# One software pipeline over all 64 units of an attention network, with the output product two slots later and the norms spread over slots

## The chip, the cores and the metric

The kernel runs on one core of a Trainium2 chip. The metric is the time of one execution on the device in microseconds, the median of several runs. The engines of the core are TensorE (PE: matmuls; PEld: its weight loads), VectorE (DVE), ScalarE (ACT), GpSimd (POOL) and SyncE (SP), whose queue issues most DMAs. Each engine works through its own queue in program order and waits on semaphores that others count up.

## The reference

The input x has 32 x 64 tokens of width 256. The first network (L0) applies two layers of cross attention with 16 heads of dimension 128, then an MLP; the second network (L1) is a smaller attention block with an MLP. The change concerns the two attention layers of L0:

```python
h = layer_norm(x)                     # mean and variance over the 256
qh = (h @ wq + bq)                    # 16 heads of 128, for 64 tokens of a batch
kh = (ctx @ wk + bk); vh = (ctx @ wv + bv)
kh, vh = concat(kh, bias_k), concat(vh, bias_v)      # 65 keys
weights = softmax(qh . kh / sqrt(128))
x = x + (weights @ vh) @ wo + bo
```

Both layers take ctx from the same context; the second layer's norm needs the first one's x, and the MLP's norm the second one's.

## The kernel before

All arithmetic is float32. A wide product is made of three matmuls on fp32r pieces (helper `three`, L166 to L170: hi x hi, hi x lo, lo x hi), so every operand exists as a rounded part (HI) and a rest (LO). `SRC_HI/SRC_LO[:, 0]` hold the transposed context, `[:, 1]` the transposed, normed x.

A **unit** is one pair of heads for one group of four token tiles (512 tokens). A layer has 8 pairs x 4 groups = 32 units, L0 has 64. One unit passes these steps: project Q and K (24 matmuls of 512 columns, PE), copy them with their bias into QT and KT (ACT, L492, L496); project V (`values(0)`, `values(1)`, 24 matmuls of 256 columns), copy it (ACT, L500), add the bias difference (POOL, L332); **scores**, 32 matmuls on 128x64 tiles into the logits (PE, L433); maximum and subtraction (DVE, L606, L615), exponential (ACT, L524), sum, reciprocal, multiply and 32x32 transposes into PRT (DVE, L567 to L578); **weigh**, 64 matmuls on 64x64 tiles of V with PRT (PE, L404) into banks 3 and 4; split into CHI (ACT, L513) and CLO (DVE, L596); **output**, 24 matmuls with wo into banks 3 and 4 again (PE), added into X (DVE, L625).

The order is written out by hand in a function `slot` for each engine. A slot has a front (unit n) and a back (unit n-1). TensorE's order is Q and K (n), values(0), weigh (n-1), values(1), scores (n), output (n-1). VectorE's is: softmax of n-1, norm, rounding of the next weights, CLO of n-1, maximum and subtraction of n, X additions of n-1. A function `slots` calls it for one layer: the first slot of a layer has no back, the last no front, so each layer ends in a drain and starts with an empty pipeline.

Weights of a pair are double buffered: SP loads W (`load`), DVE rounds it to WHI (`round_set`, L631, in slots with g = 1, where g is the group), POOL computes WLO, DV and the row sums of the output bias (`split`, L310 to L320, same slots; counted in `w_split`, for which SP's next load waits). Before the last unit of each group, POOL adds a bias row to X (L343).

The layer norm of a group of X works by stats (DVE, L88 to L97), square root (ACT, L109), reciprocal and scaling into XN (DVE, `norm_apply`, L128), transposes (PE, `norm_turn`, L137), scaling and offset from the buffer CUR into HT and SRC_HI (ACT, `norm_scale`, L152), and SRC_LO (POOL, `norm_lo`, L163). Groups 0 to 2 of the next layer's norm run in the last slots of a layer; `turning` says in which. The last group runs in slot 0 of the layer, for the MLP in the MLP's own stage.

Of the kernel before, what the change touches and what calls it, by code (L numbers as in the profile page):

```python
# [5 lines left out]
ALU = mybir.AluOpType  # L6
# [18 lines left out]
UNITS = HP * G  # L25
# [16 lines left out]
OLD = 8  # L42


def program(nc, x, ctx_in, mask, wall, vrow, borow, vech, vecm, b_fc2, qw, kw, vw, ow, out_b, w1, w2, b2, out):
    es = ExitStack()
    with es:
# [22 lines left out]
        rs = sb("rs", [P, NT])  # L70
        XN = sb("XN", [P, 2, GT, D])
# [5 lines left out]
        class Norm:  # L77
            def __init__(self, tag, src, rms, eps, prm):
                self.src, self.rms, self.eps, self.prm = src, rms, eps, prm
                self.stat, self.sqrt, self.rstd = sem(tag + "_stat"), sem(tag + "_sqrt"), sem(tag + "_rstd")  # L80
                self.xn, self.turned, self.scaled = sem(tag + "_xn"), sem(tag + "_turned"), sem(tag + "_scaled")
                self.full, self.lo = sem(tag + "_full"), sem(tag + "_lo")
                self.stats = GT if rms else 2 * GT + 1
# [56 lines left out]
        def norm_scale(e, n, k, g, banks):  # L140

            for c in range(DC):
# [5 lines left out]
                for dst, done in ((HT[:, c, :], n.full), (SRC_HI[:, 1, c, g * GTOK:(g + 1) * GTOK], n.scaled)):  # L148
                    if n.rms:
                        i = e.activation(dst, banks[c][:, :], ACT.Copy, scale=n.prm[:, c:c + 1])  # L150
                    else:
                        i = e.activation(dst, banks[c][:, :], ACT.Identity, scale=n.prm[:, c:c + 1],  # L152
                                         bias=n.prm[:, 2 + c:3 + c])
                    i.then_inc(done, 1)
# [17 lines left out]
        CUR = sb("CUR", [P, 4])  # L172

# [10 lines left out]
        norm = Norm("ln", X, False, LN_EPS, CUR)  # L184


        with ExitStack() as ph:
# [32 lines left out]

            LASTP = OLD - G

# [8 lines left out]
            cur_set = sem("cur_set")  # L231
# [7 lines left out]
            def turning(L, at, last):  # L239


                if at == 0:
                    return L, G - 1
                if last and at > LASTP + 1:
                    return L + 1, at - LASTP - 2
                return None

            def slots(e, L, slot):

                slot(L, L * UNITS, 0, L * HP, None, False)
                for i in range(0, UNITS // OLD - 1):
                    for u in range(OLD):
                        slot(L, L * UNITS + i * OLD + u + 1, u + 1, L * HP + i * 2 + (u + 1) // G, i * 2 + u // G, False)
                i = UNITS // OLD - 1
                for u in range(OLD):
                    slot(L, L * UNITS + i * OLD + u + 1, u + 1,
                         L * HP + i * 2 + (u + 1) // G if u < OLD - 1 else None, i * 2 + u // G, True)  # L260

            with nc.Block() as block:  # L262
# [27 lines left out]
                def _(e):  # L290
# [33 lines left out]
                    def slot(L, n, at, pair, hp, last):  # L324
                        g, a = at % G, (at // G) % 2
                        front, norm_now = pair is not None, turning(L, at, last)
                        if front:
                            for j in range(2):

                                e.wait_ge(v_out, 2 * n + j + 1)  # L330
                                vs = V[at % 2][:, 2 * j:2 * j + 2, :]
                                e.tensor_tensor(vs, vs, DV[a][:, :].unsqueeze(1).to_broadcast([P, 2, 2 * K]),  # L332
                                                ALU.add).then_inc(v_shift, 1)
                            if g == 1:
                                split(pair + 1, 1 - a)
                        if norm_now is not None:
                            norm_lo(e, norm, *norm_now)
                        if last and at >= G and front:

                            e.wait_ge(row_set, L + 1)  # L340
                            e.wait_ge(x_settled, 2 * n)
                            xs = X[:, (at - G) * GT:(at - G + 1) * GT, :]
                            e.tensor_tensor(xs, xs, ROW[:, :].unsqueeze(1).to_broadcast([P, GT, D]),  # L343
                                            ALU.add).then_inc(bo_added, 1)
# [4 lines left out]
                    for L in range(0, NL):  # L349
                        slots(e, L, slot)  # L350

                @block.tensor
                def _(e):
                    def slot(L, n, at, pair, hp, last):
                        g, a, ab = at % G, (at // G) % 2, ((at - 1) // G) % 2
                        front, back = pair is not None, hp is not None
                        toks = slice(g * GTOK, (g + 1) * GTOK)
                        norm_now, bridge = turning(L, at, last), last and at > LASTP
                        if front:
# [3 lines left out]
                            if at < G:  # L363

                                e.wait_ge(norm.lo, (L * G + at + 1) * DC)
                            for j, half, done, free in ((0, 1, q_done, v_out), (1, 0, k_done, k_out)):
                                if j == 1 and norm_now is not None:

                                    e.wait_ge(norm.scaled, (norm_now[0] * G + norm_now[1]) * DC)
                                if j == 1 and at == 1:  # L370
                                    e.wait_ge(norm.scaled, (L + 1) * G * DC)
                                for h in range(2):
                                    if back:

                                        e.wait_ge(free, 2 * n - 1 + h)
                                    for c in range(DC):
                                        i = three(e, PROJ[2 * j + h][:, :], WHI[a][:, j, c, h * K:(h + 1) * K],
                                                  WLO[a][:, j, c, h * K:(h + 1) * K], SRC_HI[:, half, c, toks],
                                                  SRC_LO[:, half, c, toks], c == 0, c == DC - 1)
                                    i.then_inc(done, 1)  # L380
                        def values(j):

                            e.wait_ge(q_out, 2 * n + j + 1)
                            for p in range(2):
                                t = g * GT + 2 * j + p
                                for c in range(DC):
                                    i = three(e, PROJ[j][:, p * 256:(p + 1) * 256],
                                              SRC_HI[:, 0, c, t * P:(t + 1) * P], SRC_LO[:, 0, c, t * P:(t + 1) * P],
                                              WHI[a][:, 2, c, :], WLO[a][:, 2, c, :], c == 0, c == DC - 1)
                            i.then_inc(v_done, 1)  # L390

                        if front:
                            values(0)
                        if back:

                            e.wait_ge(v_shift, 2 * n)
                            e.wait_ge(pt_out, n)
                            e.wait_ge(x_settled, 2 * n)
                            for j in range(2 * GT):
                                h, p = j // GT, j % GT  # L400
                                for dims in (slice(0, S), slice(S, P)):
                                    for b in range(2):
                                        keys = slice(b * S, (b + 1) * S)
                                        i = e.matmul(bank[3 + b][dims, j * S:(j + 1) * S],  # L404
                                                     V[(at - 1) % 2][keys, p, h * K + dims.start:h * K + dims.stop],
                                                     PRT[keys, j, :], start=True, stop=True)
                                        if j == 2 * GT - 1 and dims.start:
                                            i.then_inc(c_done, 1)
                        if front:
                            values(1)  # L410
                        if at == 0:

                            e.wait_ge(k_out, 2 * n + 2)
                            norm_turn(e, norm, *norm_now, PROJ[2:])
                        if front:

                            e.wait_ge(q_out, 2 * n + 2)
                            e.wait_ge(k_out, 2 * n + 2)
                            if g == 0:
                                e.wait_ge(kb_set, pair + 1)  # L420
                            if back:
                                e.wait_ge(sub_done, n)
                            if last and at == G - 1:

                                e.wait_ge(ones_set, 1)
                                e.wait_ge(row_acc, NL + 2 * HP * (L + 1))
# [904 lines left out]
```

## Time and profile before

| | |
|---|---|
| median of 3 runs | 1415.94 us (1415.51 to 1418.8) |
| profiled execution | 1415.35 us |
| its span, first to last instruction | 1413.2 us |
| mean granted TensorE clock | 0.976 |
| first network's attention, TensorE | 35 to 969 us |
| MLP of the first network and second network | 969 to 1413 us |

The span is from the first to the last instruction on the slowest (here the only) core; the rest of the execution's time lies around it. Times in rows are in us from the start of the span.

### The profile page before, as it was taken

The numbers are of one execution on the slowest core, as the hardware profiler recorded it, in microseconds if no ns is written. First come the engines' busy times: TensorE is split into PE (matmuls) and PEld (weight loads), VectorE is DVE, ScalarE is ACT, GpSimd is POOL, SyncE is SP. The second block draws the span as 40 slices with busy tenths as digits, with TensorE's granted clock in tenths as the row PEclk, the third lists the DMA queues.
The fourth block names the chain that finished last, engine by engine and source line by source line (L and its number), as shares of the span: only waits on it lengthen the run. The fifth ranks groups of instructions, "written<-read, shape, count | busy, mean of one in ns | idle before, by whom it ended". The sixth has DMA issues, their size and how long they took to land. (4 is left out here: it accounts for less than half of the span.)

```text
span 1413.2 us, 33171 instructions
## 1 busy us (share of the span) xinstructions
PE 1334.0 (94%) x14427; PEld 1189.8 (84%) x14427; DVE 904.8 (64%) x1792; ACT 611.8 (43%) x1045; POOL 587.3 (42%) x521
## 2 busy tenths in 40 slices
PE   3999999999999799999999999987998999997898
PEld 3898888888888688888888888977887989996787
DVE  6567767676767866767666767685323588886322
ACT  3534343434444554343434444364223256665421
POOL 4524334144144543414414324364651055554654
PEclk8999999999999999999999999997999999998999
DMA  7011011011010101101101011000000000002000
GB/s 241 4 36 39 1 39 39 1 38 39 1 39 2 38 1 39 39 2 38 38 2 39 2 38 38 2 1 27 1 1 8 1 2 2 2 2 64 4 31 30
DMA packets 31764, 35.91 MB, mean 25 GB/s; under 512 B 955, under 2 KB 29187, under 8 KB 31619
## 3 DMA queue, kind: packets, MB, share of 16 engines
q1 hardware_dynamic: 31394, 33.70, 7.6%
q8 instruction: 114, 1.87, 0.6%
q14 instruction: 30, 0.25, 0.1%
q10 hardware_dynamic: 226, 0.10, 0.0%
HBM read 31.70 MB, written 2.10 MB: 24 GB/s over the span
## 5 line engine op out<-in xcount | busy, mean ns | idle before, releaser
L332 POOL TENSOR_TENSOR V<-V,DV 128x512 f32<-128x512 f32 x128 | 164.0, 1281 | 534.5 <-ACT V L500 534.5
L168 PE MATMUL bank<-SRC_HI,WHI 128*128 128x512 f32 x576 | 230.2, 400 | 4.3 <-PEq L262 4.3
L169 PE MATMUL bank<-SRC_LO,WHI 128*128 128x512 f32 x576 | 229.4, 398 | 0.0
L170 PE MATMUL bank<-SRC_HI,WLO 128*128 128x512 f32 x576 | 228.8, 397 | 0.0
L578 DVE STREAM_TRANSPOSE PRT<-PR 32x256 f32<-32x256 f32 x512 | 223.2, 436 | 8.3
L596 DVE TENSOR_TENSOR CLO<-bank,CHI 128x512 fp32r<-128x512 f32 x128 | 82.4, 686 | 135.9 <-ACT CHI L513 135.9
L492 ACT ACTIVATE QT<-bank,PB 128x512 f32<-128x512 f32 x128 | 87.8, 688 | 177.8 <-PE bank L170 177.8
L168 PE MATMUL bank<-WHI,CHI 128*128 128x256 f32 x512 | 152.0, 297 | 4.4 <-DVE CLO L596 4.0
L168 PE MATMUL bank<-WHI,SRC_HI 128*128 128x256 f32 x512 | 150.4, 294 | 0.0
L170 PE MATMUL bank<-WHI,CLO 128*128 128x256 f32 x512 | 145.1, 283 | 0.7 <-issue 0.7
L169 PE MATMUL bank<-WLO,CHI 128*128 128x256 f32 x512 | 144.9, 283 | 0.0
L169 PE MATMUL bank<-WLO,SRC_HI 128*128 128x256 f32 x512 | 143.9, 281 | 0.0
L170 PE MATMUL bank<-WHI,SRC_LO 128*128 128x256 f32 x512 | 143.9, 281 | 0.0
L168 PEld LDWEIGHTS bank<-SRC_HI,WHI 128*128 128x128 f32 x576 | 109.5, 190 | 27.0 <-POOL SRC_LO L163 4.5
L170 PEld LDWEIGHTS bank<-SRC_HI,WLO 128*128 128x128 f32 x576 | 109.2, 190 | 26.4
L169 PEld LDWEIGHTS bank<-SRC_LO,WHI 128*128 128x128 f32 x576 | 109.6, 190 | 21.9
L496 ACT ACTIVATE KT<-bank,PB 128x512 f32<-128x512 f32 x128 | 88.4, 691 | 89.9 <-PE bank L170 89.9
L625 DVE TENSOR_TENSOR X<-X,bank 128x512 f32<-128x512 f32 x128 | 88.0, 687 | 57.9 <-PE bank L170 57.9
L500 ACT ACTIVATE V<-bank 128x512 f32<-128x512 f32 x128 | 76.5, 597 | 79.5 <-PE bank L170 79.5
L168 PEld LDWEIGHTS bank<-WHI,CHI 128*128 128x128 f32 x512 | 98.2, 192 | 9.7 <-DVE CLO L596 5.8
L168 PEld LDWEIGHTS bank<-WHI,SRC_HI 128*128 128x128 f32 x512 | 96.1, 188 | 7.2
L169 PEld LDWEIGHTS bank<-WLO,SRC_HI 128*128 128x128 f32 x512 | 96.5, 188 | 2.7
(170 smaller groups left out, 3009.7 us busy)
## 6 DMA issues: line engine op xcount, KB each, us to landing
W<-in_wall SPq DMA_DIRECT2D x18, 1024.0 KB, 5.6
VROW<-in_vrow SPq DMA_DIRECT2D x18, 256.0 KB, 6.1
V<-in_ctx SPq DMA_DIRECT2D x4, 512.0 KB, 5.8
X<-in_x SPq DMA_DIRECT2D x4, 512.0 KB, 6.8
mlp_w<-in_w SPq DMA_DIRECT2D x2, 1024.0 KB, 7.7
out<-X SPq DMA_DIRECT2D x4, 512.0 KB, 2.9
BO<-in_borow SPq DMA_DIRECT2D x1, 256.0 KB, 7.0
W<-in_qw SPq DMA_DIRECT2D x1, 256.0 KB, 4.3
```

The source lines that it names most:

```text
L168: e.matmul(dst, a_hi, b_hi, start=start, stop=False, **kw)
L169: e.matmul(dst, a_hi, b_lo, start=False, stop=False, **kw)
L170: return e.matmul(dst, a_lo, b_hi, start=False, stop=stop, **kw)
L332: e.tensor_tensor(vs, vs, DV[a][:, :].unsqueeze(1).to_broadcast([P, 2, 2 * K]), ALU.add).then_inc(v_shift, 1)
L492: e.activation(QT[:, h, :], PROJ[h][:, :], ACT.Identity, bias=PB[a][:, 0, h:h + 1]).then_inc(q_out, 1)
L496: e.activation(KT[:, h, :, 0:S], PROJ[2 + h][:, :].rearrange("p (q k) -> p q k", k=S), ACT.Identity, bias=PB[a][:, 1, h:h + 1]).then_inc(k ...
L500: e.activation(V[at % 2][:, 2 * j:2 * j + 2, :], PROJ[j][:, :].rearrange("p (t n) -> p t n", n=256), ACT.Copy).then_inc(v_out, 1)
L578: i = e.transpose(PRT[b * S + z:b * S + z + 32, :, y:y + 32], PR[b * S + y:b * S + y + 32, :, z:z + 32])
L596: e.tensor_tensor(of_batch(CLO, b), by_tile(b), of_batch(CHI, b).bitcast(F32), ALU.subtract).then_inc(c_lo, 1)
L625: e.tensor_tensor(xs, xs, bank[3 + j][:, :].rearrange("p (t n) -> p t n", n=256), ALU.add).then_inc(x_settled, 1)
```

## The change

`slots`, `turning` and CUR are gone. Every engine runs one loop `for n in range(UNITS + 2)` with UNITS = 64 (PER = 32 units a layer) across both layers. In slot n, TensorE does Q and K of unit n, output of unit n-2, the transposes of a norm, values(0), values(1) and scores of unit n, and weigh of unit n-1. Slots 64 and 65 have no front.

VectorE starts a slot with maximum and subtraction of n-1 (they stood at the end of the slot before), then CLO of n-2, `round_set` (now in slots with g = 2), the norm's reciprocal, the rest of the softmax of n-1, the X additions of n-2, and stats of a norm. ScalarE starts with CHI of n-2 and the exponential of n-1, then Q, K, the norm's scaling, V, and the norm's square root. GpSimd does the bias row of X, the norm's scaling into XN (new: `norm_apply_pool`, as X times rstd plus a shift, which VectorE prepares by a small operation, `norm_shift`), `split` (now in slots with g = 2), `norm_lo`, and the V additions. `normed(n)` and `turned(n)` give the norm group whose stats and whose rest stand in slot n: stats of group 3 of the first norm in slot 0; of groups 0 to 3 of the second layer's norm in slots 30 to 33; of groups 0 to 2 of the MLP's norm in slots 62 to 64; the rest one slot later.

```diff
+        def norm_shift(e, n, k, g):
+
+            e.wait_ge(n.rstd, k * G + g + 1)
+            ts = slice(g * GT, (g + 1) * GT)
+            e.scalar_tensor_tensor(nm[:, ts], mv[:, ts, 0], -1.0, rs[:, ts], ALU.mult, ALU.mult).then_inc(n.shift, 1)
+
+        def norm_apply_pool(e, n, k, g, shifts):
+
+            e.wait_ge(n.shift, shifts)
+            e.wait_ge(n.turned, (k * G + g - 1) * DC)
+            for p in range(GT):
+                t = g * GT + p
+                i = e.tensor_scalar(XN[:, g % 2, p, :], n.src[:, t, :], rs[:, t:t + 1], nm[:, t:t + 1],
+                                    ALU.mult, ALU.add)
+            i.then_inc(n.xn, 1)
...
+            def normed(n):
+
+                if n == 0:
+                    return 0, G - 1
+                k, g = (n + 2) // PER, (n + 2) % PER
+                return (k, g) if k >= 1 and g < G and (k, g) != (NL, G - 1) else None
+
+            def turned(n):
+                return normed(n - 1) if n >= 1 else None
...
+                        if turned(n) is not None:
+                            norm_apply_pool(e, norm, *turned(n), shifts(*turned(n)))
+                        if n < UNITS and g == 2:
+                            split(pair + 1, 1 - a)
+                        if turned(n) is not None:
+                            norm_lo(e, norm, *turned(n))
+                        if n < UNITS:
                             for j in range(2):
...
+                    def weigh(u):
+
+                        e.wait_ge(v_shift, 2 * u + 2)
+                        e.wait_ge(pt_out, u + 1)
+                        if u >= 1:
+                            e.wait_ge(x_settled, 2 * u)
...
+                    def slot(n):
+                        g, pair, L = n % G, n // G, n // PER
+                        if n < UNITS:
                             if g == 0:
 
                                 e.wait_ge(w_split, pair + 1)
...
+                            if n % PER < G:
+
+                                e.wait_ge(norm.lo, (L * G + g + 1) * DC)
                             for h in range(2):
...
+                                project(n, 0, 1, q_done, v_out, h)
+                            if n == 0:
+                                e.wait_ge(norm.scaled, (G - 1) * DC)
+                            elif turned(n - 1) is not None:
+
+                                k, q = turned(n - 1)
+                                e.wait_ge(norm.scaled, (k * G + q + 1) * DC)
+                            for h in range(2):
+                                project(n, 1, 0, k_done, k_out, h)
+                        if n >= 2:
+                            output(n - 2)
+                        if turned(n) is not None:
+
+                            if n < UNITS:
+                                e.wait_ge(k_out, 2 * n + 2)
...
+                            norm_turn(e, norm, *turned(n), PROJ[2:])
+                        if n < UNITS:
+                            values(n, 0)
+                            values(n, 1)
+                            scores(n)
+                        if 1 <= n <= UNITS:
+                            weigh(n - 1)
+
```

## Rows read from the trace of the kernel before

**Rows 1.** The page: busy time of each engine, share of the span, instructions.

```profile
PE 1334.0 (94%) x14427; PEld 1189.8 (84%) x14427; DVE 904.8 (64%) x1792; ACT 611.8 (43%) x1045; POOL 587.3 (42%) x521
```

**Rows 2.** Stretches: window, length, busy time of each engine, granted clock, DMA share, GB/s.

```profile
200.00:400.00 200.00, 199.59 (x2387) 177.77 (x2386) 139.98 (x252) 81.44 (x129) 69.88 (x64) 1.00 0.07 21
480.00:520.00 40.00, 30.64 (x285) 27.23 (x284) 26.48 (x71) 22.55 (x35) 14.90 (x11) 0.87 0.00 1
```

**Rows 3.** Timeline, PE, layer end: start, length, instruction, [idle before and its end].

```profile
466.02 1.09 PE L137 MATMUL bank<-ident,XN 128*128 128x128 f32 x8 [2.20 <-DVE XN L128]
...
491.57 1.99 PE L404 MATMUL bank<-PRT,V 64*64 64x64 f32 x64 [6.01 <-DVE PRT L578]
495.57 0.58 PE L168 MATMUL bank<-WHI,CHI 128*128 128x256 f32 x1 [2.01 <-DVE CLO L596]
...
499.15 0.34 PE L169 MATMUL bank<-WLO,CHI 128*128 128x256 f32 x1
...
520.38 1.16 PE L404 MATMUL bank<-PRT,V 64*64 64x64 f32 x64 [1.48 <-issue]
```

**Rows 4.** Timeline, PE, scores of three slots in a row.

```profile
114.49 1.15 PE L433 MATMUL logits<-KT,QT 128*64 128x65 f32 x32
...
128.54 1.15 PE L433 MATMUL logits<-KT,QT 128*64 128x65 f32 x32
...
142.39 1.15 PE L433 MATMUL logits<-KT,QT 128*64 128x65 f32 x32
```

**Rows 5.** Timeline, PE, around one weigh.

```profile
208.91 0.28 PE L170 MATMUL bank<-WHI,SRC_LO 128*128 128x256 f32 x1
209.11 1.16 PE L404 MATMUL bank<-PRT,V 64*64 64x64 f32 x64
210.21 0.39 PE L168 MATMUL bank<-WHI,SRC_HI 128*128 128x256 f32 x1
210.43 0.28 PE L169 MATMUL bank<-WLO,SRC_HI 128*128 128x256 f32 x1
```

**Rows 6.** Timeline, DVE, two slots, the second beside GpSimd's split.

```profile
106.41 0.69 DVE L571 TENSOR_TENSOR PR<-ex,ri 128x512 f32<-128x512 f32 x1
...
110.75 1.23 DVE L631 CAST WHI<-W 128x2048 fp32r<-128x2048 f32 x1
...
120.26 1.84 DVE L571 TENSOR_TENSOR PR<-ex,ri 128x512 f32<-128x512 f32 x1
122.14 3.58 DVE L578 STREAM_TRANSPOSE PRT<-PR 32x256 f32<-32x256 f32 x8
```

**Rows 7.** Timeline, POOL: a split, and a norm_lo.

```profile
116.51 5.05 POOL L310 TENSOR_TENSOR WLO<-W,WHI 128x512 fp32r<-128x512 f32 x4
...
122.68 1.82 POOL L318 TENSOR_SCALAR tmp<-W,PH 128x256 f32<-128x256 f32 x2
...
124.61 1.61 POOL L303 TENSOR_TENSOR acc<-acc,tmp 128x256 f32<-128x256 f32 x2
...
933.75 3.10 POOL L163 TENSOR_TENSOR SRC_LO<-HT,SRC_HI 128x512 fp32r<-128x512 f32 x2 [3.50 <-ACT SRC_HI L152]
```

**Rows 8.** Timeline, ACT: a table load, and CHI in the last drain.

```profile
944.16 1.28 ACT L524 ACT_TABLE_LOAD   x1
...
956.69 1.09 ACT L513 ACTIVATE CHI<-bank 128x512 fp32r<-128x512 f32 x2 [6.49 <-PE bank L404]
```

**Rows 9.** Timeline, PE: turns of the last drain, first matmul of the MLP.

```profile
944.37 1.09 PE L137 MATMUL bank<-ident,XN 128*128 128x128 f32 x8
...
963.75 1.03 PE L137 MATMUL bank<-ident,XN 128*128 128x128 f32 x8
...
969.12 0.77 PE L168 MATMUL bank<-SRC_HI,WHI 128*128 128x512 f32 x1 [4.34 <-PEq L262]
```

**Rows 10.** Timeline, DVE: CLO and the end of the stats in the last drain.

```profile
957.32 1.29 DVE L596 TENSOR_TENSOR CLO<-bank,CHI 128x512 fp32r<-128x512 f32 x2 [2.76 <-ACT CHI L513]
...
960.39 0.16 DVE L97 TENSOR_TENSOR ms<-mv,ms 128x4 f32<-128x4 f32 x1
```

More of the change, by code:

```diff
@@ L24 @@
 GTOK = TOK // G
-UNITS = HP * G
+UNITS = NL * HP * G
+PER = HP * G
 F = 1024
@@ L183, in program @@
         w_hi, w_split = sem("w_hi"), sem("w_split")
-        norm = Norm("ln", X, False, LN_EPS, CUR)
+        norm = Norm("ln", X, False, LN_EPS, [PM[:, k * LNP:k * LNP + 4] for k in range(NL + 1)])
         with ExitStack() as ph:
@@ L237, in program, with shifts @@
             p_ready, x_settled = sem("p_ready"), sem("x_settled")
[L239 to L260, printed above, removed]
+            def normed(n):
[5 more added lines that the diff above has]
+                return normed(n - 1) if n >= 1 else None
+            def shifts(k, g):
+                return k * G + g - (G - 1) + 1
             with nc.Block() as block:
@@ L336, in slot @@
[L336 to L344, printed above, removed]
@@ L348, in _, with project @@
                         norm_lo(e, norm, 0, g)
-                    for L in range(0, NL):
-                        slots(e, L, slot)
+                    for n in range(UNITS + 2):
+                        slot(n)
                 @block.tensor
                 def _(e):
-                    def slot(L, n, at, pair, hp, last):
-                        g, a, ab = at % G, (at // G) % 2, ((at - 1) // G) % 2
-                        front, back = pair is not None, hp is not None
+                    def project(n, j, half, done, free, h):
+                        a, g = n // G % 2, n % G
@@ L357, in slot @@
                         toks = slice(g * GTOK, (g + 1) * GTOK)
-                        norm_now, bridge = turning(L, at, last), last and at > LASTP
-                        if front:
+                        if n >= 1:
+                            e.wait_ge(free, 2 * n - 1 + h)
+                        for c in range(DC):
+                            i = three(e, PROJ[2 * j + h][:, :], WHI[a][:, j, c, h * K:(h + 1) * K],
+                                      WLO[a][:, j, c, h * K:(h + 1) * K], SRC_HI[:, half, c, toks],
+                                      SRC_LO[:, half, c, toks], c == 0, c == DC - 1)
@@ new lines, in output @@
+                    def output(u):
+                        a = u // G % 2
+                        e.wait_ge(c_lo, 2 * u + 2)
+                        for j in range(2):
+                            for p in range(2):
+                                ts = slice((2 * j + p) * P, (2 * j + p + 1) * P)
+                                dst = bank[3 + j][:, p * 256:(p + 1) * 256]
+                                for h in range(2):
+                                    i = three(e, dst, CHI[:, h, ts], CLO[:, h, ts], WHI[a][:, 3, h, :],
+                                              WLO[a][:, 3, h, :], h == 0, h == 1)
+                            i.then_inc(o_done, 1)
@@ L360, in slot @@
+                    def slot(n):
+                        g, pair, L = n % G, n // G, n // PER
+                        if n < UNITS:
                             if g == 0:
                                 e.wait_ge(w_split, pair + 1)
[L363 to L408, printed above, removed]
@@ L548, in _ @@
                     norm_scale(e, norm, 0, 2, PROJ[2:])
-                    for L in range(0, NL):
-                        slots(e, L, slot)
+                    for n in range(UNITS + 2):
+                        slot(n)
                 @block.vector
@@ L589, in slot @@
-                        if front and g == 1:
-                            round_set(pair + 1, 1 - a)
-                        if back:
-                            for b in range(2):
-                                e.wait_ge(c_hi, 2 * n - 1 + b)
-                                e.tensor_tensor(of_batch(CLO, b), by_tile(b), of_batch(CHI, b).bitcast(F32),
-                                                ALU.subtract).then_inc(c_lo, 1)
-                        if norm_now is not None and not front:
-                            e.wait_ge(x_settled, 2 * n)
-                            norm_stats(e, norm, *norm_now)
-                            norm_rstd(e, norm, *norm_now)
-                            norm_apply(e, norm, *norm_now)
@@ L658, in _ @@
                     e.wait_ge(x_in[G - 1], 16)
-                    e.memset(mx[:, :], 0.0).then_inc(x_settled, 2)
-                    for L in range(0, NL):
-                        slots(e, L, slot)
+                    for n in range(UNITS + 2):
+                        slot(n)
         def mlp(tag, norm, k, b1, w, ready, b2d, func, dst, more):
```

253 lines of the change are left out of this document (126 added, 127 removed).

## The prediction

> **What bounds the kernel now.** I read the busy shares first: TensorE is busy 94% of the span, VectorE 64%, ScalarE 43%, GpSimd 42% [rows 1]. Busy TensorE is no proof of work at full rate, so I then cut the span into stretches. Inside a layer TensorE is busy 199.6 of 200 us at full clock, with VectorE at 140; around 500 us it is busy 30.6 of 40 at a mean granted clock of 0.87 [rows 2], a mix of the two levels, 2.4 and 1.2 GHz. So TensorE sets the pace, and what can be won in the first network is idle time and half clock at the layer ends, and whatever small gaps hide in the slots. Third, the idle times noted at TensorE's own instructions give the places and who ended them: the biggest is 6.01 us ahead of weigh (L404) for the transposed probabilities PRT at 491.57, and the same again in the second layer [rows 3]. Last, the starts of scores (L433) show the beat: 13.85 us a slot [rows 4].
>
> **The slots inside a layer.** The 144 wide matmuls of a unit are the same. Two small groups interrupt them: weigh (64x64 tiles) and scores (128x64 tiles). Around weigh, the step from the last 256-wide matmul is 0.20 us where its neighbours need 0.12 (0.08 lost), and the first wide matmul after it takes 0.22 (0.10 lost) [rows 5]; scores shows the same pattern. So a slot holds two entries and two exits, 0.37 us together. In the new order scores and weigh stand back to back: one entry, one exit, and one step between two small tile shapes, which the trace of before never shows. Its price has bounds from these rows: 0 if nothing is lost between them, 0.19 if it costs what entry plus exit cost now; both tile shapes start from already small matmuls, nearest to a single entry or exit, so I take 0.10. The gain is then 0.09 to 0.10 us in each of 62 full slots: 6 us (0 to 12). The row shows 0.08 to 0.10 us lost at every change of tile shape. The Trainium skill, TensorEngine Tiling, Key Properties, says that a change of tiling mode drains TensorE; the trace agrees with 0.08 to 0.10 us each, and by that rule three changes a slot in place of four would give the same 6 us.
>
> One slot of four takes 14.05 instead of 13.85 us [rows 4]. There GpSimd's split runs beside VectorE's PR multiply, which takes 1.84 us instead of 0.69, and the eight transposes (3.58 us) end at 125.72 and hold weigh up by the 0.2 us [rows 6]. In the new order weigh(n-1) stands at the end of slot n. The chain there, from slot start: CHI copies and the last CLO subtraction until 2.0, (round_set in slots with g = 2, to 3.3), sum, reciprocal and multiply until 4.7 (5.9 beside the split), transposes until 8.3 (9.5), and weigh wants them at 12.5. So this wait goes and nothing is late next: 16 x 0.2 = 3.3 us. The split itself moves from g = 1 to g = 2, needed first at the next g = 0, 14 us after it ends, and the weight DMAs that SP issues behind w_split start one slot later with two slots still to spare, so I cost that at nothing. Also output(n-2) wants CLO at 5.6 us into the slot (after Q and K) and has it at 2.0; its cover is 3.6 us.
>
> **The middle drain.** Before: TensorE idles 6.01 us for PRT, runs weigh in 1.99 instead of 1.16 us, idles 2.01 us for CLO, and runs the first 17 matmuls of output at 0.21 us a step instead of 0.12, until 499.15 [rows 3]. That is 6.0 + 0.8 + 2.0 + 1.6 = 10.4 us, all gone, as units 29 to 31 are finished beside units 31 to 33. Refilling costs 1.48 us in the second slot of a layer (L404 at 520.38, and as much at 56.04) since weigh comes before VectorE has PRT [rows 3]: 3.0 us gone, by the same 12.5 us schedule.
>
> **The norms.** Before, a turn waits for XN in the slot: 2.20 us at 466.02 [rows 3], and for the other three some 0.2 us, with 0.3 us for CLO behind each of the four, as VectorE does stats, root and scaling in one go ahead of CLO: 2.2 + 0.6 + 1.2 = 4.0 us gone. In the new order stats end slot n, and reciprocal and shift (two operations of some 0.2 us) stand behind CLO in slot n+1. GpSimd does the scaling: four 128x256 operations. Nearest row: its tensor_scalar of that size, 1.82 us for two [rows 7], so 3.7 us (if two scalars cost twice, 7.3). From 2.5 (shift) or 3.2 (behind the bias row) it ends at 6.9, and the turn comes at 8.4 behind Q, K and output: hidden by 1.5 us. In slot 1, where there is no output, the turn comes at 5.6 and XN at some 5.7: 0.2 us lost, up to 1.5; I take 0.5. ScalarE loads its table twice per norm (1.28 us each [rows 8]), at slot ends, under cover of the 3.6 us above.
>
> **A new wait.** Slot 34 is both turned(34) = (1, 3) and g = 2. GpSimd's order there is apply, split, norm_lo, then the V shifts, and slot 35 begins with Q, which waits for norm_lo of this group; all of TensorE stands behind it. Worked out from slot 34's start: CLO until 2.0, round_set 1.23 [rows 6], reciprocal and shift until 4.0 with a margin; apply 3.7 to 7.7; split from 116.51 to 126.22 = 9.7 us (its rows begin at the first and end with the last, 124.61 + 1.61) to 17.4; norm_lo 3.1 us [rows 7] (2.6 at best) to 20.5. Slot 34 with its turn (0.9) lasts 14.6. So TensorE idles 5.9 us, and after as long an idle time it restarts at the lower clock: 2.4 us as in the middle drain (0.8 + 1.6). Loss 8.3 us (7.5 to 9.5). No other slot has both: the turns are in slots 1, 31 to 34 and 63 to 65.
>
> **The last drain.** Before: from turn(2,1) at 944.37 to the first matmul of the MLP at 969.12 it takes 24.75 us [rows 9]. What is left then is turn(2,1), output(62), weigh(63), output(63), turn(2,2): just what slots 64 and 65 hold. The new chain: CHI, table load and Exp until 3.2 (1.1 + 1.28 + 0.64, with 0.2 of handing over), sum to transposes 5.2 more, 8.4; the two X additions, for which weigh(63) waits by x_settled, 1.4, 9.8; weigh at half clock 2.0, 11.8; ScalarE stands in sqrt(2,2) until the stats that follow the X additions are done (2.0, as from CLO's end at 958.6 to 960.55 [rows 10], then 0.5) at 12.3; CHI 1.09 [rows 8] and the last CLO 0.7 [rows 10], with 0.3, 14.4; output(63) at the lower clock 4.7, 19.1; and from the turn to the MLP 969.12 - 963.75 = 5.4 [rows 9], 24.5. Equal, within 3 us either way.
>
> **The sum.** Gains 6 + 3.3 + 10.4 + 3.0 + 4.0 = 26.7; losses 8.3 + 0.5 = 8.8; tail 0. Net 17.9 us. The profiled execution took 1415.35 us (span 1413.2), and the median of the runs is 1415.94, 0.6 above. 1415.35 - 17.9 = 1397.4, and 1398 against the median.
>
> **The rivals.** (a) The split does not stall slot 35, because apply and stats come so much earlier or TensorE's order leaves it slack: 1398 - 8 = 1390. Against: the GpSimd queue is in order, and the split's rows alone fill 9.7 of 14.6 us. (b) GpSimd's scaling is slow: at 7.3 us the turn of slots 31 to 34 and 63 comes at some 10.5 instead of 8.4, 2.1 us each, slot 1 4 us, and slot 34 pushes slot 35 by 3.6 more: 10.5 + 4 + 3.6 = 18, 1416: within noise of no gain. For: beside VectorE, GpSimd's own times vary (norm_lo 3.1 and 2.6 for two). (c) Slower: the step from scores to weigh, a change between two small tile shapes that the trace of before has nowhere, costs far more than a change from wide matmuls. Gain without the shape term is 12 us; it is eaten up when the step costs 12/62 + 0.19 = 0.38 us, and at 0.6 us the kernel takes 1398 + 6 + 62 x 0.41 = 1429. Against: all four changes seen cost 0.10 or less. (d) The change doesn't do what it says: the layer boundary still idles, since Q of slots 32 to 34 waits for norm_lo. Slot 32 wants it at 14.6; the turn starts at 8.4, and turn, scalings, norm_lo and the start of the next stage took 5.4 before [rows 9], 13.8: only 0.8 us to spare. If it misses by 2 us in three slots: 1404.
>
> **How the numbers follow.** Forecast as summed, 1398: 0.68, its own range 1391 to 1406 by the shape term (6 either way), the new stall (1) and the tail (3), not all at once. (a) 1390: 0.10. (d) 1404: 0.09. (b) 1416: 0.08. (c) 1429: 0.05. A range of 1387 to 1408 holds the forecast, (a) and (d) nearly whole, 0.83, and leaves (b) and (c) out. A measurement of this kernel can tell 0.3% (4.2 us) from no change: faster, under 1411.7, is forecast, (a), (d) and a sliver of (b): 0.88; same 0.07; slower 0.05.
>
> **What would show it.** Right: L404's waits for PRT in the middle are gone; scores beat every 13.75 us with no slot of 14.05; one wait of 5 to 7 us of TensorE at slot 35 for GpSimd's SRC_LO, with half clock behind it; the clock near 1.0 across 480 to 520 us; about 25 us from slot 63's end to the MLP. Wrong: waits of TensorE for XN (apply on GpSimd too slow), for CLO at each output (the two-slot delay not enough), a beat above 13.85, or no wait at slot 35.

## The result and the profile after

The changed kernel takes 1384.39 us, the median of 4 runs (1383.21 to 1386.07), against 1415.76 us for the kernel before in the same comparison: a ratio of 0.9775, 95% interval 0.976 to 0.9791. That is 31.4 us less, where 18 were forecast, and below the range's low end of 1387. Its profiled execution took 1383.66 us with a span of 1381.7.

The page of the changed kernel, busy time by engine, then TensorE's busy tenths and granted clock in 40 slices:

```profile
PE 1311.4 (95%) x14427; PEld 1181.0 (85%) x14427; DVE 881.0 (64%) x1764; ACT 605.8 (44%) x1047; POOL 603.3 (44%) x553
...
PE   3999999999999999999999999978989999996898
...
PEclk8999999999999999999999999999999999999999
```

The same two stretches as [rows 2], columns as there:

```profile
200.00:400.00 200.00, 200.00 (x2503) 181.09 (x2502) 137.32 (x255) 79.86 (x131) 75.20 (x70) 1.00 0.07 24
480.00:520.00 40.00, 36.75 (x471) 32.85 (x470) 31.84 (x73) 25.86 (x40) 28.64 (x30) 0.96 0.11 34
```

Around 500 us TensorE's busy time rises from 30.64 to 36.75 of 40 us and the granted clock from 0.87 to 0.96. In the first stretch the idle time was 0.41 us before and is nothing now. Over 14 slots that is 0.03 us a slot, while the slots got shorter by 0.22 us, as the next rows show. So most of what was won inside a layer was never idle time in the trace: it lay in the starts of instructions. (The counts, 2387 matmuls before and 2503 now, do not measure it: a slot holds 168 in both kernels, and the second window happens to hold a 15th pair of the small groups of 32 and 64.)

TensorE's timeline around the end of a slot in the changed kernel (L404 is scores, L419 weigh, L185 the first of the three matmuls), which answers to [rows 5]:

```profile
206.00 0.28 PE L187 MATMUL bank<-WHI,SRC_LO 128*128 128x256 f32 x1
206.21 1.15 PE L404 MATMUL logits<-KT,QT 128*64 128x65 f32 x32
207.29 1.16 PE L419 MATMUL bank<-PRT,V 64*64 64x64 f32 x64
208.38 0.50 PE L185 MATMUL bank<-SRC_HI,WHI 128*128 128x512 f32 x1
208.72 0.39 PE L186 MATMUL bank<-SRC_LO,WHI 128*128 128x512 f32 x1
...
219.84 1.15 PE L404 MATMUL logits<-KT,QT 128*64 128x65 f32 x32
```

From scores to scores it is 13.63 us, against 13.85 in [rows 4], and no fourth slot is longer any more. Scores take 1.08 us from their start to the next group's start, here with weigh behind them, and before with a wide matmul behind them.

**Where the 31.5 us are.** The MLP's first matmul starts at 937.63 instead of 969.12 [rows 9], 31.5 us earlier, the whole difference of the spans. The table is worked out from the starts of scores of every unit. Its last two rows leave out one weigh (1.2 us with its changes of tile shape), which stood ahead of scores and now stands behind them:

| | before | after | won |
|---|---|---|---|
| 62 slots from unit 1 to unit 63, at their beat | 13.85 | 13.63 | 13.6 |
| 0.2 us more in each fourth slot | 3.3 | 0 | 3.3 |
| layer ends up to unit 63: drain, refill, norm turns | 20.3 | 4.4 (5 turns of 0.88) | 15.9 |
| slot 35 | | 4.6 | -4.6 |
| one idle time of 0.66 us without a releaser and what lies round it, at 596.77 in the trace of before alone | 0.9 | 0 | 0.9 |
| start of the loop to slot 1 | | | 1.2 |
| last scores to the MLP, same work counted | 26.0 | 25.3 | 0.8 |

The rows add up to 31.1 us; of the rest 0.1 us lies in slots 3 to 5, which took 13.88 to 13.91 us before. GpSimd at slot 34 of the changed kernel: scaling (L129), split (L313 to L306), norm_lo (L180):

```profile
501.21 2.59 POOL L129 TENSOR_SCALAR XN<-X,rs,nm 128x256 f32<-128x256 f32 x4 [2.22 <-DVE nm L121]
503.77 5.02 POOL L313 TENSOR_TENSOR WLO<-W,WHI 128x512 fp32r<-128x512 f32 x4
508.75 0.73 POOL L316 TENSOR_TENSOR DV<-VROW 128x256 f32<-128x256 f32 x1
...
511.38 1.59 POOL L306 TENSOR_TENSOR acc<-acc,tmp 128x256 f32<-128x256 f32 x2
512.93 2.50 POOL L180 TENSOR_TENSOR SRC_LO<-HT,SRC_HI 128x512 fp32r<-128x512 f32 x2
```

and TensorE, behind it, at the first matmul of slot 35:

```profile
515.49 0.80 PE L185 MATMUL bank<-SRC_HI,WHI 128*128 128x512 f32 x1 [3.25 <-POOL SRC_LO L180]
```

The forecast wait is there, at the place and with the releaser it was given, but 3.25 us long and not 5.9. Scores of units 34 and 35 show what it costs:

```profile
509.99 1.15 PE L404 MATMUL logits<-KT,QT 128*64 128x65 f32 x32
...
528.24 1.15 PE L404 MATMUL logits<-KT,QT 128*64 128x65 f32 x32
```

That step is 18.25 us, 4.6 over the beat. TensorE's last drain has five waits in 24 us; four of them stand in the chain that the prediction worked out, and the 1.35 us for XN do not:

```profile
915.39 0.38 PE L185 MATMUL bank<-WHI,CHI 128*128 128x256 f32 x1 [2.02 <-DVE CLO L590]
919.82 1.06 PE L154 MATMUL bank<-ident,XN 128*128 128x128 f32 x8 [1.35 <-POOL XN L129]
923.79 1.44 PE L419 MATMUL bank<-PRT,V 64*64 64x64 f32 x64 [2.91 <-DVE X L621]
927.80 0.58 PE L185 MATMUL bank<-WHI,CHI 128*128 128x256 f32 x1 [2.57 <-DVE CLO L590]
932.30 1.03 PE L154 MATMUL bank<-ident,XN 128*128 128x128 f32 x8
937.63 0.47 PE L185 MATMUL bank<-SRC_HI,WHI 128*128 128x512 f32 x1 [4.29 <-PEq L265]
```

### The profile page after: what moved, and what is told of

Same layout as the page of the kernel before. It is cut to its first block and busy times, and to the rows that moved or that the text cites. A ratio compares the mean times of both kernels' runs of the same rounds, so it can differ in the third digit from the quotient of the medians.

```text
span 1381.7 us, 33156 instructions
## 1 busy us (share of the span) xinstructions
PE 1311.4 (95%) x14427; PEld 1181.0 (85%) x14427; DVE 881.0 (64%) x1764; ACT 605.8 (44%) x1047; POOL 603.3 (44%) x553
## 5 line engine op out<-in xcount | busy, mean ns | idle before, releaser
L185 PE MATMUL bank<-SRC_HI,WHI 128*128 128x512 f32 x576 | 235.7, 409 | 7.5 <-PEq L265 4.3
L566 DVE TENSOR_REDUCE mx<-logits 128x8 f32<-128x520 f32 x64 | 44.7, 699 | 193.0 <-PE logits L404 192.7
L185 PE MATMUL bank<-WHI,CHI 128*128 128x256 f32 x512 | 144.9, 283 | 4.6 <-DVE CLO L590 4.6
L185 PE MATMUL bank<-WHI,SRC_HI 128*128 128x256 f32 x512 | 144.5, 282 | 0.0
L185 PEld LDWEIGHTS bank<-SRC_HI,WHI 128*128 128x128 f32 x576 | 109.7, 190 | 33.6 <-POOL SRC_LO L180 7.9
L187 PEld LDWEIGHTS bank<-SRC_HI,WLO 128*128 128x128 f32 x576 | 109.2, 190 | 25.3
L313 POOL TENSOR_TENSOR WLO<-W,WHI 128x512 fp32r<-128x512 f32 x68 | 92.3, 1388 | 61.3 <-DVE WHI L631 61.3
L510 ACT ACTIVATE CHI<-bank 128x512 fp32r<-128x512 f32 x128 | 69.6, 596 | 92.0 <-PE bank L419 91.5
L185 PEld LDWEIGHTS bank<-WHI,CHI 128*128 128x128 f32 x512 | 97.2, 190 | 7.6 <-DVE CLO L590 4.9
```

The source lines that it names most:

```text
L185: e.matmul(dst, a_hi, b_hi, start=start, stop=False, **kw)
L187: return e.matmul(dst, a_lo, b_hi, start=False, stop=stop, **kw)
L313: i = e.tensor_tensor(WLO[a][:, j, :, :], W[a][:, j, :, :], WHI[a][:, j, :, :].bitcast(F32), ALU.subtract)
L510: e.activation(of_batch(CHI, b), by_tile(b), ACT.Copy).then_inc(c_hi, 1)
L566: e.tensor_reduce(mx[:, :].rearrange("p (h t) -> p h t", h=2), logit, AX_X, ALU.max).then_inc(mx_done, 1)
```

## The experiments

Two questions were open: why a slot gains twice what was forecast, and whether the layer end and slot 35 are what the forecast took them for. Each kernel was timed beside the kernel before, on the chip of its group (medians 1415.76, 1415.08 and 1417.24 us); ratios are to those.

**The small groups apart again.**

```diff
                             values(n, 0)
-                            values(n, 1)
                             scores(n)
+                            values(n, 1)
                         if 1 <= n <= UNITS:
                             weigh(n - 1)
```

> The changed kernel with one matmul group moved: scores stands between values(0) and values(1), weigh stays at the end of the slot. The two small groups are then apart again, with two entries from wide matmuls and two exits; nothing waits earlier than before. Theory A (a small group costs 0.08 us at its entry from wide matmuls and 0.10 to 0.11 us at its exit, and the step from one small group to the other is free): the slot goes from 13.63 back to 13.84 us, 62 x 0.2 = 12 to 13 us more, some 1397 us. Rival B (the 0.22 us a slot came from something else in the new order, such as hidden waits in the old place of weigh or output): the slot stays at 13.63 us and the time at 1384 to 1386 us.

Measured: 1399.91 us, ratio 0.9888 (0.9873 to 0.9903), 15.5 us more than the changed kernel. TensorE's timeline:

```profile
206.09 1.15 PE L404 MATMUL logits<-KT,QT 128*64 128x65 f32 x32
207.17 0.39 PE L185 MATMUL bank<-WHI,SRC_HI 128*128 128x256 f32 x1
...
208.79 1.16 PE L419 MATMUL bank<-PRT,V 64*64 64x64 f32 x64
209.88 0.50 PE L185 MATMUL bank<-SRC_HI,WHI 128*128 128x512 f32 x1
...
219.93 1.15 PE L404 MATMUL logits<-KT,QT 128*64 128x65 f32 x32
```

The slot is 13.84 us, the old beat to 0.01 us, with everything else of the new pipeline in place. The gain per slot comes from scores and weigh being neighbours; rival B is out. The beat gives 62 x 0.21 = 13 us; slot 35 costs another 1.9 here (its wait is 3.9 us in this trace). That the step between the small groups is free is not shown by this, and the next run denies it.

**The small groups in four pieces.** `scores` and `weigh` get an argument for the head:

```diff
-                            scores(n)
-                        if 1 <= n <= UNITS:
-                            weigh(n - 1)
+                        for h in range(2):
+                            if n < UNITS:
+                                scores(n, (h,))
+                            if 1 <= n <= UNITS:
+                                weigh(n - 1, (h,))
```

> The changed kernel with scores and weigh cut in halves by head and interleaved: scores head 0, weigh head 0, scores head 1, weigh head 1. The same matmuls, but three steps between the two small tile shapes in a slot instead of one. Theory A (steps between small shapes are free): slot 13.63 us, time 1384 to 1386 us. Rival C (the prediction's price, about 0.10 us at every change of tile shape, hidden in the changed kernel by something else): two more changes a slot, 63 x 0.2 = 13 us more, some 1397 us.

Measured: 1407.0 us, ratio 0.9937 (0.992 to 0.9954), 22.6 us more than the changed kernel: Theory A is wrong, and rival C's figure, 0.10 us a change, is too small. TensorE's timeline (here L422 is weigh):

```profile
209.75 0.69 PE L404 MATMUL logits<-KT,QT 128*64 128x65 f32 x16
210.37 0.70 PE L422 MATMUL bank<-PRT,V 64*64 64x64 f32 x32
211.00 0.69 PE L404 MATMUL logits<-KT,QT 128*64 128x65 f32 x16
211.61 0.69 PE L422 MATMUL bank<-PRT,V 64*64 64x64 f32 x32
212.24 0.50 PE L185 MATMUL bank<-SRC_HI,WHI 128*128 128x512 f32 x1
```

Half a group takes 0.62 us from start to start, a whole one 1.08 to 1.09. So a piece costs 0.16 us that does not depend on its size, and 0.47 us for each half of the matmuls. That 0.16 us was inside the durations of scores and weigh all along, where I had read only work. It could be the price of the change of tile shape, or of a new piece with its semaphore waits. Two more kernels tell these apart.

**The same pieces without the changes of shape.** scores head 0, scores head 1, weigh head 0, weigh head 1, with the repeated waits.

> A control for the four pieces: the same halves with the same repeated semaphore waits, but in the order scores head 0, scores head 1, weigh head 0, weigh head 1, so that only one step changes the tile shape. Theory E (the 0.16 us of a piece is the price of the change of tile shape): slot 13.63 us, 1384 to 1386 us. Rival F (it is the price of the repeated waits, or of any new piece of small matmuls): as slow as the four pieces, slot 13.99 us, 1407 us.

Measured: 1382.6 us (1381.58 to 1384.33), ratio 0.9756 (0.9736 to 0.9775), level with the changed kernel.

```profile
205.31 1.15 PE L404 MATMUL logits<-KT,QT 128*64 128x65 f32 x32
206.40 1.16 PE L422 MATMUL bank<-PRT,V 64*64 64x64 f32 x64
...
218.94 1.15 PE L404 MATMUL logits<-KT,QT 128*64 128x65 f32 x32
```

The slot is 13.63 us, and the halves of a kind flow into one another. Rival F is out.

**The interleaved pieces without repeated waits.**

> The four interleaved pieces (scores head 0, weigh head 0, scores head 1, weigh head 1) with the semaphore waits only ahead of the first piece of each kind. Theory E (the change of tile shape costs 0.16 us): slot 13.95 to 13.99 us, 1404 to 1407 us, as with the repeated waits. Rival F (the repeated waits cost it): slot 13.63 us, 1384 to 1386 us. In between, 0.04 us a slot or 2.5 us in all could belong to the waits, as the sum of the pieces gave 0.32 us a slot where 0.36 was measured.

Measured: 1407.4 us (1402.88 to 1408.52), ratio 0.9919 (0.9891 to 0.9947). Here L405 is scores and L424 weigh:

```profile
210.38 0.69 PE L405 MATMUL logits<-KT,QT 128*64 128x65 f32 x16
210.99 0.69 PE L424 MATMUL bank<-PRT,V 64*64 64x64 f32 x32
...
224.36 0.69 PE L405 MATMUL logits<-KT,QT 128*64 128x65 f32 x16
```

The slot is 13.98 us, 0.35 over 13.63 for two more changes of shape, waits or none. Theory E holds: the price belongs to the change of tile shape, 0.16 to 0.18 us for each change between the two small ones. A small group costs 0.16 us inside its span; coming to it from wide matmuls costs 0.09 us more (a late start), going back to wide ones 0.11 (their second start is late). The four changes in a slot of the kernel before cost 2 x (0.09 + 0.16 + 0.11) = 0.72 us, the three of the changed kernel 0.09 + 2 x 0.16 + 0.11 = 0.52: 0.20 of the 0.22 us that the beat gained.

The halves don't say where in the span the 0.16 us lie. The single starts in the trace of the changed kernel do: the pairs of scores' matmuls start every 0.06 us, but the second pair 0.11 us behind the first (0.05 late), and weigh starts 0.15 us behind the last matmul where 0.05 is the rule (0.10 late). Weigh shows the same. Counted so, a change costs 0.14 us from wide to small (0.09 + 0.05), 0.15 between the small ones (0.10 + 0.05) and 0.20 from small to wide (0.10 + 0.10). That scores and weigh also differ in operands and banks is no likely rival: from output to V, which differ in both but share the wide shape, the step is 0.12 us, as within each.

The Trainium skill says (TensorEngine Tiling, Key Properties) that a change of tiling mode drains TensorE. These runs agree in that every change costs time; that it is a drain they do not show, and the page gives no figure.

**The small groups swapped.** `weigh(n - 1)` ahead of `scores(n)`, both behind values(1).

> The changed kernel with the two small groups swapped: weigh(n-1), then scores(n), at the end of the slot. Still one entry, one step between small shapes, one exit. The four-piece run showed 0.16 us per group of small matmuls that does not depend on how many it holds. Theory A (every change of tile shape costs, whichever way it goes; the last one before wide matmuls costs most): slot stays at 13.63 us, 1384 to 1385 us. Rival D (the price of the step depends on its direction, from the 64x64 to the 128x64 tiles): the slot moves by 0.05 to 0.2 us, 3 to 12 us in all. That scores end 1.1 us later is covered by some 3 us in both theories.

Measured: 1384.88 us, ratio 0.9778 (0.9757 to 0.98); the slots start every 13.63 us, so the order of the two is of no account to the beat, and rival D is out. Only slot 35 differs in its trace, 20.46 us in place of 18.25, with a wait of 3.96 us for norm_lo.

**norm_lo ahead of the split.**

```diff
+                        if turned(n) is not None:
+                            norm_lo(e, norm, *turned(n))
                         if n < UNITS and g == 2:
                             split(pair + 1, 1 - a)
-                        if turned(n) is not None:
-                            norm_lo(e, norm, *turned(n))
```

> The changed kernel with GpSimd's norm_lo ahead of its split in the one slot (34) that has both. If TensorE's wait at the start of slot 35 is due to norm_lo standing behind split, the 3.25 us of waiting and the 1.4 us of lower clock behind it go: scores of unit 35 follow those of 34 after 13.6 us instead of 18.25, and the kernel takes 4.6 us less, 1379.8 us. Rival: the split, now 3 us or more later, holds up the additions to V or the next weights, and the wait only moves to weigh(34) or to slot 36: 1383 us or more.

Measured: 1378.62 us (1375.05 to 1380.6), ratio 0.9733 (0.9714 to 0.9752). GpSimd, then scores of units 34 and 35:

```profile
508.52 2.61 POOL L180 TENSOR_TENSOR SRC_LO<-HT,SRC_HI 128x512 fp32r<-128x512 f32 x2 [4.60 <-ACT SRC_HI L169]
511.10 5.02 POOL L313 TENSOR_TENSOR WLO<-W,WHI 128x512 fp32r<-128x512 f32 x4
```

```profile
510.10 1.15 PE L404 MATMUL logits<-KT,QT 128*64 128x65 f32 x32
...
523.73 1.15 PE L404 MATMUL logits<-KT,QT 128*64 128x65 f32 x32
```

The step is 13.63 us where it was 18.25: 4.62 us, of which 3.25 were the wait and 1.37 the lower clock behind it. Between 500 and 540 us TensorE now waits for nothing, so the wait was not moved on, and it was norm_lo behind the split. The changed kernel starts the scores of unit 63 at 911.12, this one at 906.61. (The spans differ by only 3.2 us, the medians by 5.8; what lies behind unit 63 varies by a microsecond or two from one execution to the next.) It is the fastest kernel of the study, 37 us under the kernel before.

**The drain put back.** A function `front_of(s)` gives slot s its unit; slots 32 and 33 have none, so that units 30 and 31 are finished alone. Every engine's loop runs over 68 slots.

```diff
+            def front_of(s):
+                if 0 <= s < PER:
+                    return s
+                return s - 2 if PER + 2 <= s < UNITS + 2 else None
...
-                        if n >= 2:
-                            output(n - 2)
+                        if back is not None:
+                            output(back)
```

> The changed kernel with the drain put back between the two layers and nothing else: two slots without a front behind unit 31 (output 30 and weigh 31, then output 31), and unit 32 starts an empty pipeline. From the last drain of the changed kernel: 19.8 us from the end of slot 63 to the end of its last turn, of which 8.5 us is work that the pipeline does anyway, so 11.3 us more. The norm of group 3 no longer meets the split, which gives back 4.6 us. Theory: 1384.4 + 11.3 - 4.6 = 1391 us. Rival (the layer end was worth little once the two small groups stand together and the norms are spread): 1386 us or less. If the stall at slot 35 is not due to the meeting with the split, 1396 us.

Measured: 1392.67 us (1390.84 to 1394.29), ratio 0.9835 (0.982 to 0.985), 8.3 us more than the changed kernel. TensorE at the drain (L427 is weigh, L412 scores):

```profile
478.82 1.99 PE L427 MATMUL bank<-PRT,V 64*64 64x64 f32 x64 [2.88 <-DVE X L632]
482.82 0.58 PE L185 MATMUL bank<-WHI,CHI 128*128 128x256 f32 x1 [2.02 <-DVE CLO L601]
...
499.59 1.15 PE L412 MATMUL logits<-KT,QT 128*64 128x65 f32 x32
...
509.33 1.15 PE L412 MATMUL logits<-KT,QT 128*64 128x65 f32 x32
```

From the scores of unit 31 to those of unit 35 it takes 70.4 us (466.15 to 536.58), in the changed kernel 61.8 (466.45 to 528.24): 8.6 us, and 13.2 with the 4.6 us of slot 35 that this kernel doesn't pay. The sum said 11.3; the refill behind the drain, with 0.78 us of waiting for KT, was not in it. So the drain with its refill is worth some 13 us.

**Output directly behind Q.** `output(n - 2)` moved ahead of the two K products.

> The changed kernel with output(n-2) moved ahead of K: directly behind Q, 2.8 us into the slot instead of 5.6. CLO is there 2.0 us after the end of weigh, so if the prediction's cover of 3.6 us is right, 0.8 us of it is left and nothing changes: slot 13.63 us, 1384 us, but for the norm slots 31 to 35, where ScalarE's square root starts CHI 0.4 to 0.5 us later and still fits. Rival: the cover is smaller than worked out and TensorE waits for CLO in each slot, 0.5 us or more each, 1415 us or more.

Measured: 1388.53 us (1386.43 to 1391.67), ratio 0.9808 (0.9784 to 0.9831), 4.1 us more. The slot is 13.61 us and no slot waits for CLO, so the cover is as worked out. What I had missed is in the wait table:

```profile
PE bank L154 <- ACT KT L521: 0.8, 1, 0.8
```

in the changed kernel, and here

```profile
PE bank L154 <- ACT KT L522: 4.7, 6, 0.8
```

A turn writes into the banks of K and so waits for ScalarE's copies of them. Output stood between K and the turn and covered it; without it each of six turns waits 0.8 us. (Slot 35 gave back 0.7 us of it, with a wait of 2.3 us in place of 3.3.) This is the wait of slot 1 of the changed kernel too, which has no output, and there it took the place of the wait for XN that the prediction named.

**One part alone in the kernel before.** `weigh` moved behind `values(1)`, ahead of `scores`; output still in the same slot.

> The kernel before with one part alone of the change: weigh(n-1) moved behind values(1), directly ahead of scores(n), output(n-1) still in the same slot, layers still drained. Theory: the gain per slot of the two groups together cannot be had without the output two slots later. One fewer change of tile shape gives 0.22 us a slot, and weigh, 1.4 us later, no longer waits in each fourth slot (3.3 us); but output wants CLO 1.1 us behind weigh's end and has it after 2.0, so TensorE waits 0.9 us in each of 62 slots: 1415.8 - 13.6 - 3.3 + 56 = 1455 us. Rival (the old order had cover for it, the output's place is of no account): 1399 us.

Measured: 1460.69 us, ratio 1.0314 (1.0295 to 1.0333), 45.6 us slower than before. TensorE's waits:

```profile
PE bank L168 <- DVE CLO L594: 57.4, 60, 2.0
```

57.4 us in 60 waits, a slot of 14.7 us. With the output in its old place the two neighbours cost more than they gain: the output two slots later is what makes room for them. Whether another order gives the same room was not tried.

**The norm's scaling back on VectorE.** `norm_apply_pool` dropped, `norm_apply` behind VectorE's reciprocal.

> The changed kernel with the norm's scaling into XN back on VectorE (1.4 us behind the reciprocal) instead of GpSimd (2.2 to 2.6 us). All the rest as in the changed kernel, split ahead of norm_lo too. GpSimd can then start slot 34's split when the rounded weights are there, at 500.8 instead of 503.8 us, and norm_lo ends 3 us earlier: TensorE's wait at slot 35 falls from 3.25 to about 0.3 us and the lower clock behind it goes, 4.3 us less; VectorE's transposes end 1.2 us later, under 3 us of cover. Theory: 1380 us, and the moved scaling was a loss of its own. Rival (VectorE becomes late in the norm slots, and weigh or CLO wait for it): 1384 us or more.

Measured: 1384.64 us (1382.56 to 1387.54), ratio 0.978 (0.9758 to 0.9802): no difference, so the theory's 4 us did not come. VectorE and GpSimd in slot 34:

```profile
501.97 5.30 DVE L145 TENSOR_SCALAR XN<-X,mv,rs 128x256 f32<-128x256 f32 x4
```

```profile
501.93 5.18 POOL L313 TENSOR_TENSOR WLO<-W,WHI 128x512 fp32r<-128x512 f32 x4 [2.52 <-DVE WHI L629]
```

Beside GpSimd's split, VectorE's four scalings take 5.30 us instead of 1.38 (487.56 in the same trace, no split beside them), and GpSimd loses almost nothing. TensorE's waits from 470 to 540 us show what came of it:

```profile
PE bank L417 <- DVE X L619: 1.5, 1, 1.5
PE bank L154 <- DVE XN L145: 0.7, 1, 0.7
```

The wait for norm_lo is gone and two others stand in its place: slots 34 and 35 take 15.38 and 15.27 us in place of 14.51 and 18.25, which gives back 2.1 us; and in the last drain weigh waits 5.3 us for X instead of 2.9, which takes them again.

## Why the prediction was wrong

The direction, the places and most mechanisms were right. The gain was 31.4 us where 17.9 were summed. Two terms were mis-sized, both the same way, and make up 11.3 of the 13.5 us between: the price of a change of tile shape (7.6) and the wait at slot 35 (3.7). The idle time of 0.66 us in the trace of before (0.9) and the last drain (0.8, taken at nothing) make up most of the rest.

- **The price of a change of tile shape** is the term that failed most: 6 us forecast (0 to 12), 13.6 measured. The working put a whole small group at 0.18 us beside its matmuls, from the gaps around it [rows 5], and the step between two small shapes at 0.10 us on top of two groups' durations. The rows of the four pieces put a group at 0.36 us and a change between small shapes at 0.16: both figures were too small, for the same reason, as 0.16 us of each group lie inside the 1.08 us that I took for the matmuls' own time. What counts is the difference, an exit and an entry saved: 0.20 us where 0.09 to 0.10 was taken. To the two durations that were there before, the step between the small groups adds nothing; that was the lower end of its bounds (0), and would have given 12. The last 0.02 us a slot (1.2 us in all) are not explained by the rows, and stay open. Rival (c), that this step costs far more than a change from wide matmuls, is out.
- **The wide matmuls** of a unit are 72, three times 24, and not 144; the sum did not use the number.
- **The fourth slots**, 3.3 us: right. 16 slots lost 0.2 us each and none does now.
- **The middle drain, one refill and the norm waits**: 10.4 + 1.5 + 4.0 = 15.9 us at the layer ends, and 15.9 in the table. To the tenth this is luck: the drain put back costs 13.2 us where drain and refill were taken at 11.9, which leaves 2.7 us for the norm waits, not 4.0. The other refill belongs to the start of the loop, where 1.2 us came in all.
- **The new wait at slot 35**: right in place and cause, shown by the run with norm_lo ahead, but 4.6 us instead of 8.3 (7.5 to 9.5). GpSimd's four scalings took 2.59 us, not 3.7 (the row taken, tensor_scalar with one scalar at 0.92 us each, is slower than the operation itself with 0.65), and started 0.5 us earlier; the split took 9.2, not 9.7; norm_lo 2.5, not 3.1. So each term was taken at the slow end of its rows, and the wait was 3.25 us, not 5.9. The lower clock behind it cost 1.4 us, not 2.4; that part varies between executions, as 1.4 to 2.9 us were lost behind waits of 2.3 to 4.0 us at this place in the other traces, and the shorter wait is no reason for it.
- **Slot 1**: 0.5 us forecast, for XN; 0.78 came, for KT. The step "the turn comes at 5.6" had left out ScalarE's copies.
- **The last drain**: worked out as 24.5 us from the end of slot 63; 913.3 to 937.63 is 24.3. The chain's waits are in the trace in the order given. Some parts cancel: weigh starts after 10.5 us and not 9.8, but takes 1.4 us and not 2.0.
- **Rivals**: (a) is out, as slot 35 waits; (b) is out, GpSimd's scaling takes 2.2 to 2.6 us; (d) is out, slots 31 to 34 take 14.51 us each, which is the beat and a turn of 0.88.
- **The range**: the forecast's own ended at 1391, and 1387 was chosen to hold rival (a). Both errors (7.6 and 3.7 us) went beyond their own bounds (6 and 1) and the same way, and a range that took its bounds as met "not all at once" had no room for their sum.

## What to carry to other kernels

A wait table shows idle time, not the price of what stands next to what: where an engine is busy all the time, compare the starts of consecutive instructions, and split a group in halves to find the part of its time that does not shrink. Put matmuls of the same or similar small tiles side by side, and look first for the delay that gives them the room. When work is spread over an in-order queue, look for the one slot in which two pieces meet, and put the one that somebody waits for first.

## What the runs showed of the hardware

- A change of tile shape on TensorE costs 0.16 to 0.18 us between 128x64 and 64x64 tiles by the slot of the four pieces, in either direction. By the single starts it is 0.15 us between the small shapes, 0.14 from wide (128x128) to small and 0.20 from small to wide. Of the 0.36 us around one small group only 0.09 (its late start) and 0.11 (the late second wide start) stand outside its own time; 0.16 lie inside it.
- VectorE's tensor_scalar on 128x256 float32 took 0.35 us each alone and 1.33 beside GpSimd's subtraction on SBUF tiles, nearly four times as much, while GpSimd's took 1.30 instead of 1.26. In the kernel before, the multiply by a broadcast took 1.84 instead of 0.69 in the same company [rows 6]. The Trainium skill (GPSIMD Engine Reference, Specifications) says that the two engines share SBUF interfaces, and contend when VectorE runs in a 2-port mode or reads two SBUF inputs. The traces agree that they contend, and show that in these pairs VectorE pays nearly all of it; in which mode it ran they do not show.
- Behind the wait of 3.25 us at slot 35 TensorE's granted clock was at its lower level, 1.2 GHz: wide matmuls started every 0.43 us instead of 0.23 from 515.49 until 518.22, which cost 1.4 us on top of the wait. At the same place in other runs a wait of 2.3 us (output directly behind Q) was followed by the lower clock too and cost 1.7 us more, one of 3.0 us (interleaved pieces, no repeated waits) 2.7 more, one of 4.0 us (small groups swapped) 2.9 more. So the price of the clock did not simply grow with the wait, and a wait of 3 us cost 4.6 or 5.7 us in all.
